# A second place for one batch's score operand, and a new order of the start, in a fused post-norm decoder layer

## The reference, cut to what matters

```
# 1: squared-relu attention against fixed keys (4 heads of 64, 1024 keys)
n = layernorm(x) * g + b
p = square(relu(einsum('bhtd,sd->bhts', n_heads, k)));  x = LN(x + (x + einsum(p, v)))
# 2: cross attention to ctx (16 heads of 16) with a clipped bias from frac
attn = gamma*QK^T/4 + delta*(ap*max(D,0) + an*min(D,0));  x = LN(x + softmax(attn) V Wo + bo)
# 3: feed-forward 256 -> 1024 -> 256; the top one of 8 experts adds its rank-4 LoRA before the relu
x = LN(x + relu(x wi + wi_b + lora_e(x)) wo + wo_b)
```

## Time and profile before

| | us |
|---|---|
| median of 3 runs | 902.18 (898.16 to 902.9) |
| the profiled execution | 896.02 |
| its span in the profile | 894.2 |
| busy: PE, DVE, ACT, POOL | 839.8, 760.4, 716.8, 587.9 |
| first matrix product of the scores starts at | 18.27 |
| first product of batch 1's scores | 40.52 |
| first logits of batch 0 | 66.16 |

### The profile page before, as it was taken

How to read it: one execution, slowest core, us unless ns; L and a number is a source line. 1 busy time by engine, 2 the same in 40 slices (tenths; PEclk the granted TensorE clock), 3 DMA queues, 4 the chain that set the end, 5 groups by cost and what they waited for, 6 DMA issues and landing times.

```text
span 894.2 us, 20601 instructions
## 1 busy us (share of the span) xinstructions
PE 839.8 (94%) x7012; PEld 667.6 (75%) x7012; DVE 760.4 (85%) x2158; ACT 716.8 (80%) x1949; POOL 587.9 (66%) x762
## 2 busy tenths in 40 slices
PE   2787989999999999999999999999999999999866
PEld 1354757878888787887877787788878787788766
DVE  4778889989898898989889898989889798899842
ACT  3568899888897988888897988889798888889821
POOL 2867776776767686776777586776768676544310
PEclk9999999999999999999999999999999999999998
DMA  6223323222132222223123222213222221313100
GB/s 173 86 51 55 65 38 62 38 46 41 43 67 58 43 49 54 43 56 58 43 42 72 37 43 54 54 43 50 64 42 48 50 49 24 77 22 53 31 12 23
DMA packets 40025, 46.12 MB, mean 52 GB/s; under 512 B 10257, under 2 KB 27153, under 8 KB 39922
## 3 DMA queue, kind: packets, MB, share of 16 engines
q1 hardware_dynamic: 39922, 44.82, 25.1%
HBM read 15.42 MB, written 4.19 MB: 22 GB/s over the span
## 4 chain that ended last, share of the span: by engine, by line
PE 87%; ACT 6%; DVE 3%; issue 2%; POOL 1%; POOLq 0%; DVEq 0%; ACTq 0%
PE bank L226 21%; PE bank L270 12%; PE bank L351 12%; PE bank L415 10%; PE bank L364 7%; PE bank L258 6%; PE bank L342 6%; PE bank L259 6%; ACT P L564 2%; PE bank L422 2%; PE bank L290 1%; ACT STG L489 1%; ACT R L510 1%; PE bank L376 1%; PE bank L247 1%
## 5 line engine op out<-in xcount | busy, mean ns | idle before, releaser
L988 POOL TENSOR_SCALAR U<-DP,alph 128x512 f32<-128x512 f32 x256 | 186.9, 731 | 128.4 <-DVE NM L778 72.6
L970 POOL TENSOR_TENSOR R<-R 128x512 f32<-128x512 f32 x212 | 228.0, 1076 | 64.2 <-ACT R L510 64.1
L564 ACT ACTIVATE P<-T,NM 128x256 f32<-128x256 f32 x512 | 256.3, 511 | 2.9 <-DVE NM L778 2.9
L771 DVE SCALAR_TENSOR_TENSOR bank<-DN,alph,bank 128x512 f32<-128x512 f32 x256 | 191.2, 747 | 40.8 <-PE bank L342 38.5
L778 DVE CUSTOM_DVE_ANT_0 T<-bank,U 128x256 f32<-128x256 f32 x512 | 197.0, 422 | 9.0 <-DVE bank L771 0.2
L510 ACT ACTIVATE R<-bank 128x512 f32<-128x512 f32 x256 | 152.6, 598 | 46.7 <-PE bank L259 42.3
L489 ACT ACTIVATE STG<-bank 128x512 f32<-128x512 f32 x256 | 152.4, 595 | 27.5 <-PE bank L351 25.7
L351 PE MATMUL bank<-ident,P 128*128 128x128 f32 x1024 | 155.5, 274 | 6.9 <-ACT STG L489 5.8
L351 PEld LDWEIGHTS bank<-ident,P 128*128 128x128 f32 x1024 | 117.5, 140 | 29.9 <-ACT P L564 14.7
L270 PE MATMUL bank<-R,VS 128*32 128x512 f32 x1024 | 124.1, 603 | 4.9 <-DVE R L727 3.9
L258 PE MATMUL bank<-SK,KH 128*128 128x512 f32 x256 | 115.5, 451 | 5.7 <-DVE SK L721 5.7
(11 more groups left out here) (164 smaller groups left out, 1887.7 us busy)
## 6 DMA issues: line engine op xcount, KB each, us to landing
QS<-QK SPq DMA_DIRECT2D x384, 64.0 KB, 2.3
XG<-in_x SPq DMA_DIRECT2D x16, 256.0 KB, 3.1
CT<-in_ctxT SPq DMA_DIRECT2D x16, 256.0 KB, 2.8
out<-XO SPq DMA_DIRECT2D x16, 256.0 KB, 2.5
FK<-in_frac SPq DMA_DIRECT2D x16, 128.0 KB, 3.2
STG<-in_wiT SPq DMA_DIRECT2D x2, 512.0 KB, 4.0
STG<-in_woT SPq DMA_DIRECT2D x2, 512.0 KB, 4.0
STG<-in_kT SPq DMA_DIRECT2D x2, 256.0 KB, 3.9
```

Source lines behind the costliest of these rows:

```text
L564: eng.activation(P[n % NP][:, cs], T[n % NT][:, cs], ACT.Exp, bias=NM[:, n % 8, q:q + 1], scale=-1.0, accum_out=SU[n // 16 % 2][:, q, seat ...
L771: eng.scalar_tensor_tensor(out=L[:, :], in0=dn[:, :], scalar=alph[:, 16 + h:17 + h], in1=L[:, :], op0=ALU.mult, op1=ALU.add).then_inc(s_t1, 1)
L970: eng.tensor_tensor(r[:, :], r[:, :], r[:, :], ALU.mult).then_inc(s_sqp, 1)
L988: eng.tensor_scalar(U[n % NU][:, :], dp[:, :], alph[:, h:h + 1], 0.0, ALU.mult, ALU.add).then_inc(s_u, 1)
```

## The change

Batch 1's score operand no longer goes to `SK` but to rows 2 and 3 of `IH`, which the feed-forward doesn't use before batch 0 reaches it. So `skh(1)` no longer waits for batch 0's scores. The wait of `skh(2)` becomes 16 scores (batch 0's only), and `ih` gets a wait for 32 scores. All other differences are places: `early` numbers of batch 0, and separate `if g ==` places for the start. Numbers with `late`, the places of batches 2 to 14 and the period are as before.

```diff
+        def sk(b, h):
+            if b == 1:
+                return IH[:, 2 + h, :]
+            return SK[:, h, :, :].rearrange("p a t -> p (a t)")
@@ scores, skh, skl use sk(b, h) in place of SK
-                act.wait_ge(s_sc, 16 * b)
+                act.wait_ge(s_sc, 16 * b if b > 2 else 16 * (b // 2))
@@ ih
+                act.wait_ge(s_sc, 32)
@@ tensor
-                for b, u in due(g, -1161, 16, 37, early=-8, late=1):
+                for b, u in due(g, -1161, 16, 37, early=-90, late=1):
                     scores(b, u)
-                for b, _ in due(g, -1233, early=-20, late=19):
+                if g == -1459:
+                    xnT(0)
+                if g == -638:
+                    xnT(1)
+                for b, _ in due(g, -1233, start=2, late=19):
                     xnT(b)
@@ vector
-            weight("kT", KL[:, :], stage(1024, 0), KH[:, :])
             for g in GRID:
...
-                if g == -1826:
+                if g == -1877:
                     dve.wait_ge(d_x[0], 16)
                     stats("a", 0, XG[0])
-                for b, _ in due(g, -1407, early=-205, late=70):
+                if g == -1854:
+                    centred("a", 0, XN, XG[0], s_x0)
+                if g == -1065:
+                    dve.wait_ge(s_xnT, 1)
+                    centred("a", 1, XN, XG[1], s_x0)
...
+                if g == -1360:
+                    weight("kT", KL[:, :], stage(1024, 0), KH[:, :])
@@ gpsimd
-                if g == -1955:
+                if g == -1863:
+                    pool.wait_ge(s_x0, 2)
                     eng.memset(f(QS[0][:, 0, :, :]), 0.0).then_inc(s_qz, 1)
-                if g == -377:
+                if g == -675:
                     eng.memset(f(QS[1][:, 0, :, :]), 0.0).then_inc(s_qz, 1)
@@ sync
             load_x(0)
+            spread(gB[:, :], a["ln_g"], d_ln)
+            spread(bB[:, :], a["ln_b"], d_ln)
             eng.dma_start(stage(1024, 0)[0:64, :], a["kT"]).then_inc(d_w["kT"], 16)
             eng.dma_start(stage(1024, 0)[64:128, :], a["kT"]).then_inc(d_w["kT"], 16)
-            spread(gB[:, :], a["ln_g"], d_ln)
-            spread(bB[:, :], a["ln_b"], d_ln)
```

More of the change, by code:

```diff
@@ L720, in skl @@
                     own, other = slice(64 * h, 64 * h + 64), slice(64 - 64 * h, 128 - 64 * h)
-                    eng.tensor_tensor(SK[other, h, :, :], b3[own, :, :], f(SK[own, h, :, :]),
+                    eng.tensor_tensor(sk(b, h)[other, :], bank[own, :], f(sk(b, h)[own, :]),
                                       ALU.subtract).then_inc(s_skl, 1)
@@ L872, in _ @@
+                if g == -1151:
+                    dve.wait_ge(d_x[1], 16)
+                    stats("a", 1, XG[1])
+                for b, _ in due(g, -1509, start=2, late=20):
                     dve.wait_ge(d_x[b % 2], 16 * (b // 2 + 1))
                     stats("a", b, XG[b % 2])
-                for b, _ in due(g, 666):
+                for b, _ in due(g, 666, early=-6):
                     rc(b)
-                for b, _ in due(g, 812):
+                for b, _ in due(g, 812, early=-1):
@@ L877, in _ @@
                     ao(b)
-                for b, _ in due(g, 854, early=-24, late=15):
+                for b, _ in due(g, 854, early=14, late=15):
                     aol(b)
-                for b, _ in due(g, -1232, early=-117, late=13):
+                if g == -1351:
+                    skl(0)
+                if g == -628:
+                    skl(1)
+                for b, _ in due(g, -1232, start=2, late=13):
                     skl(b)
-                for b, _ in due(g, 1636, early=-10, late=671):
+                for b, _ in due(g, 1636, early=-29, late=671):
@@ L935, in _ @@
                     ull(b)
-                for b, u in due(g, -1133, 16, 37, early=-3, late=9):
+                for b, u in due(g, -1133, 16, 37, early=-49, late=9):
                     if on_dve(b, u):
@@ L996, in _ @@
             for g in GRID:
[L997 removed]
+                for b, u in due(g, -9, 16, 41, early=10, late=-8):
                     positive(16 * b + u)
[L999 removed]
+                for b, _ in due(g, 706, early=66):
                     rx(b)
[L1001 removed]
+                for b, _ in due(g, -372, early=60, late=14):
                     rsqrt("b", b)
[L1003 removed]
+                if g == -1066:
+                    rsqrt("a", 1)
+                for b, _ in due(g, -1402, start=2, late=-9):
                     rsqrt("a", b)
[L1005 removed]
+                if g == -2424:
                     rsqrt("a", 0)
[L1007 removed]
+                if g == -789:
+                    gain(1)
+                for b, _ in due(g, -1291, start=2, late=-4):
                     gain(b)
[L1009 removed]
+                if g == -944:
                     eng.memset(gate_b[:, :], 0.0).then_inc(s_cst, 1)
@@ L1036, in _ @@
                     plus(X1b[b % 2], X1, boB, s_x1b)
-                for b, _ in due(g, 1396, early=123, late=634):
+                for b, _ in due(g, 1396, early=1, late=634):
                     pool.wait_ge(s_x2, 2 * b + 2)
@@ L1041, in _ @@
                     plus(X2b, X2, woB, s_x2b)
-                for b, u in due(g, -1087, 16, 38, early=16, late=4):
+                for b, u in due(g, -1087, 16, 38, early=-5, late=4):
                     if not on_dve(b, u):
@@ L1156, in _ @@
                                   f(IL[0:1, 0:2, :])).then_inc(d_lb, 16)
-                for b, u in due(g, 169, 4, 133, early=-23, late=-107):
+                for b, u in due(g, 169, 4, 133, early=-34, late=-107):
                     restack(4 * b + u)
@@ L1166, in _ @@
                     load_c(b)
-                for b, _ in due(g, 2434, early=424, late=754):
+                for b, _ in due(g, 2434, early=445, late=754):
                     sp.wait_ge(s_xo, 2 * b + 2)
```

209 lines of the change are left out of this document (103 added, 106 removed).

## The result

| | before | after |
|---|---|---|
| median, us (5 runs each) | 901.29 (898.16 to 902.9) | 895.43 (894.56 to 896.08) |
| ratio of the two, 95% interval | | 0.9942, 0.9917 to 0.9967 |
| span of the profiled execution, us | 894.2 | 893.6 |
| mean granted clock of that execution | 0.993 | 0.986 |

The change saves 5.9 us in the median (by the interval of the ratio, 3.0 to 7.5); 5.3 were forecast, to 896.9. But the two profiled spans differ by 0.6 us only. That contradiction is what most of the experiments are about.

What follows compares the result with a forecast made beforehand. TensorE, busy 94% of the span, was taken as the bound, so gain comes only where it waits. Start 4.6 - batch 0 2.6 + change of batch 3.3 = 5.3 us off 902.18 gives 896.9; range 892.5 to 901.5.

Steps and rivals of the forecast that it cites:

- the forecast's own signs: Marks to check: first scores 13.0 to 15.3, av(0,2) near 32.2, scores (1,0) idle under 2 us, x1(0)'s turn near 47.3.
- Start: Batch 0's first scores start at 13.7 instead of 18.27 us: 4.6 us earlier, bounds 3.0 and 5.3.
- Batch 0 gives back 2.6 of 4.6: By av(0,2), at 32.2 instead of 34.21 us, 2.6 us of the start's lead is lost; bounds 1.3 and 4.5.
- three causes of the loss: In batch 0: late output weights; gain(1) and rsqrt(a,1) ahead of needed squares; ACT's i1 and i0 between relus.
- Change of batch, 3.3 us: From av(0,2) to the end of av(0,3), 9.9 us becomes 6.6, 1.0 of the gain being the clock.
- its failure as a rival: Rival 2, change of batch: the new operand brings nothing, the stretch shrinks only 0.8; gain 2.8 us, 899.4; chance 0.15.
- The clock: Ahead of batch 1's scores: the shorter idle time keeps TensorE's clock up, worth 1.0 us of the 3.3.
- the row at 49.72: Profile row before the change: an idle time of 1.88 us followed by an av of 1.92 us, at full clock.
- rival 1: Batch 0 is POOL's and ACT's, and the clock still falls ahead of batch 1: gain 2.4 us, 899.8; chance 0.15.
- x1(0) at 47.3: Turn of x1(0) comes at 47.3 instead of 52.61 us; context rows hidden with 0.5 us to spare.
- Attention at 0: Shifts in batch 0's attention cost 0, earlier and later operations balancing; bounds a gain of 3 and a loss of 3.

Runs made afterwards that it cites:

- the run with the start alone: Kernel before with only batch 0's start (SP's queue, DVE and ACT order, memset) as in the changed kernel, all later places as before: 898.76 us.
- the changed kernel with its attention undone: Changed kernel with the places of batch 0's attention and feed-forward, the LB DMAs and gate_b's as before: 895.67 us.
- the filled kernels: Changed kernel and kernel before, each with matrix products nobody reads added at four places where TensorE waits: 891.85 us and 895.20 us.
- the attention's places alone: Kernel before with only the places of batch 0's attention and feed-forward, the LB DMAs and gate_b's as in the changed kernel: ratio 0.9998.
- the third kernel: Changed kernel with unread products at the four places and also at the start and in the last batch: 889.32 us, ratio 0.986 to before.

## Why the prediction was right, and where it wasn't

The total came out, 5.9 for 5.3, but not by the forecast's own signs. It called itself wrong if the lead at the turn of x1(0) wasn't 5.3 us or if it changed by over 1 us from there to 130 us: in the profiles it was 4.2, and 1.8 at the turn of batch 2's heads. No stretch of low clock was to be left near 38 us: there it was 0.66. So part of the agreement is luck: the executions of one kernel lie up to 8 us apart, and the medians are of five each. The chain of waits was right; the clock was not.

- **Start: 4.6 us forecast, 5.2 measured.** The steps hold with small errors: statistics from 3.67 (3.9), centring in 1.32 us (1.4), gain from 7.31 (7.6). The high keys were begun at 9.16, not 9.8, and that is the difference. Reordering SP's queue had the bytes delivered in the order of issue, as assumed.
- **Batch 0 gives back 2.6 of 4.6: it gave back 3.1 of 5.2.** av(0,2) was put at 32.2 and stands at 32.07; the first `av` at 21.7, and 21.49. But I named three causes of the loss and didn't work out what the new places save; the run with the start alone shows it, with ACT's q ahead of the first relu. How well 2.0 us of lead at av(0,2) hit is partly luck: six profiles with the new order have it at 32.1 to 32.9, and four with the old one at 34.2 to 35.5, where bias_o is slow or not.
- **Change of batch, 3.3 us.** From av(0,2) to the end of av(0,3) I had 6.6 us: with the clock up it is 32.05 to 38.66, 6.6 us, in the changed kernel with its attention undone; in the changed kernel's own profile 8.2. In the filled kernels the stretch is 8.9 before and 6.6 after, so that 2.3 are the chain and the 1.0 left of the 3.3 is the clock, which is how I had split them. The idle time is 2.10 (1.9 forecast). I had expected the new operand to be part of the cause, with its failure as a rival (15%); it is no part that these runs can tell, and yet that rival's price was wrong too, since the places do without it. Reading TensorE's order against `skh`'s wait would have told it.
- **The clock: the step that failed.** I took 1.0 us for it, as something that the shorter idle time would save, with the row at 49.72 as evidence. The same idle time of about 2 us was followed by an `av` of 3.08 us in one execution and of 1.92 in others of the same work. The longer one isn't decisive either: behind an idle time of 2.83 us the `av` took 2.89, 3.64 and 3.42 us in three profiles of the old order, and 1.92 in two (the start alone, and the attention's places alone):

```profile
40.78 0.47 PE L258 MATMUL bank<-SK,KH 128*128 128x512 f32 x1 [2.83 <-DVE SK L721]
...
41.50 1.92 PE L270 MATMUL bank<-R,VS 128*32 128x512 f32 x16
```

One row isn't a rule: what falls behind such a wait is a matter of the execution, and in sum it makes some 6 us, more than any other term. The part of rival 1 by which the clock falls at the change of batch all the same came true in the changed kernel's profile, behind 2.10 us. At equal mean clock the two kernels lie 3.3 us apart at 0.988 (894.56 and 895.03 against 897.95 and 898.2), 4.8 at 0.986, and 4.4 with both filled at 0.995. So of the median's 5.9 us, 3.3 to 4.8 are a shorter chain, where I had 4.3, and for the rest, 1 to 2.5 us, where I had 1.0, the clock falling less often or for shorter is the likely cause; no run shows how often it falls in each kernel apart from these few executions.

- **x1(0) at 47.3: at 48.44, and at 47.27 with the clock held.** The distance from the end of av(0,3) was right within 0.3 us (8.2 for 8.5), so the miss is the long `av`. What the turn waits for is ACT's queue, not the context rows.
- **Attention at 0**: shown in both directions.

The medians of the filled kernels are 3.35 us apart where their marks at the first logits are 4.4 apart (65.01 and 60.60). In the profiled execution the one fall of the clock at 108 us accounts for it: the lead falls by 1.6 us there, and not at all in the third kernel. Open is what lies between 3.3 and 4.4, since the filled kernel before was profiled with the slow products at the start (bias_o 1.05 us, first `av` at 26.42 for 25.11).

## What to carry to other kernels

Before comparing two profiles, put each execution's mean granted clock beside its time, and compare at the same clock; here 0.012 of it is 6 us, the size of the whole change. The mean doesn't tell everything: executions at 0.988 and at 0.991 took the same 898.2 us. Where TensorE waits some 2 us between dense stretches, products that nobody reads may be worth more than shortening the wait. And before giving an operand a second buffer, look whether the engine's own order already settles the wait.

## What was not expected of the hardware

- The same program on the same core takes 896.0 to 904.1 us, and the time follows the mean granted clock group by group; the difference lies at the first 170 us and the end, while from batch 3's turn to batch 13's pass 615.44 to 615.47 us in every profile.
- The same wait of 2.83 us, in the same order of work, was followed by the lower clock in three profiles and by the full one in two.
- The granted clock of the start isn't shown as low (1.00 from 8 to 20 us in the changed kernel), and yet the first twelve products of the scores are 0.43 us apart where later ones are 0.23: there the products' own times have to be read.
- DVE's two-input difference takes 1.21 us, and 2.0 to 2.3 us beside a sum or product of two operands on POOL. The Trainium skill, page "SBUF — State Buffer", section "Who interferes with whom", has a DVE instruction with two inputs in SBUF contend with a GpSimd instruction that reads SBUF; the trace agrees, 2.29 for 1.21 us. In the changed kernel the same DVE instruction started first and kept its 1.21, and the product of POOL that started 0.3 us later took 1.81 for 1.04.
- One memset of POOL under the two centrings makes them 1.32 us, two make them 2.22, where twice the median of one centring is 0.82. The second centring has its 0.4 us in both; the first takes 1.01 and 1.90, and ends 0.15 us behind the last memset in both. The Trainium skill, page "SBUF — State Buffer", section "Who interferes with whom", has the shared ports go to whoever issues first for the whole instruction, and the other blocked; the trace agrees, 0.15 us behind the memset either way.
